# One gathered tile of rows in every third chunk fetched row by row from ScalarE's queue

## The reference

```
f = (x @ W_ni.T)[src] + (x @ W_nj.T)[dst] + e @ W_fij.T
f = leaky_relu(f, negative_slope=0.2)
score = f @ attn
m = segment_max(score, dst)
a = exp(score - m[dst])
a = a / segment_sum(a, dst)[dst]
h_out = segment_sum((x @ W_node.T)[src] * a, dst)
```

## Time and profile before

| | |
|---|---|
| median of three executions | 2192.31 us |
| the profiled execution's own time | 2185.84 us |
| its span (first to last instruction) | 2184.0 us |
| PE busy | 1812.9 us (83%) |
| POOL busy | 1588.6 us (73%) |
| DVE busy | 1497.5 us (69%) |
| ACT busy | 421.8 us (19%) |
| TensorE's mean granted clock | 0.929 |
| bytes moved | 486.65 MB, mean 223 GB/s |

### The profile page before, as it was taken

One profiled execution on the slowest core, in us unless ns is written; L12 is line 12 of the kernel. 1 busy time (PEld: TensorE's weight loads), 2 busy tenths in 40 slices (PEclk: granted clock), 3 DMA queues, 4 the chain that ended last, 5 costly groups with the idle time before them and its releaser, 6 DMA issues.

```text
span 2184.0 us, 43046 instructions
## 1 busy us (share of the span) xinstructions
PE 1812.9 (83%) x10541; PEld 1243.9 (57%) x10696; DVE 1497.5 (69%) x5518; ACT 421.8 (19%) x844; POOL 1588.6 (73%) x1671
## 2 busy tenths in 40 slices
PE   5699889888888888888857788888788888878887
PEld 3366666555565666555634555555555555555566
DVE  6488888777777767777735666666666667657666
ACT  2221121111111111111111112222212222222221
POOL 7777777777777777777277777777777777777771
PEclk9899999998999889999979999999999999999988
DMA  9889998888888878888456666666666666666661
GB/s 318 258 269 279 281 288 279 260 251 250 266 253 259 253 244 263 258 255 255 141 172 189 192 200 196 195 198 196 192 199 195 195 193 200 194 189 203 195 198 44
DMA packets 349544, 486.65 MB, mean 223 GB/s; under 512 B 114284, under 2 KB 215188, under 8 KB 349454
## 3 DMA queue, kind: packets, MB, share of 16 engines
q1 hardware_dynamic: 236515, 248.47, 37.7%
q0 software_dynamic: 78752, 213.75, 33.7%
q10 hardware_dynamic: 34203, 23.55, 3.6%
HBM read 407.69 MB, written 81.38 MB: 224 GB/s over the span
## 4 chain that ended last, share of the span: by engine, by line
POOL 54%; issue 18%; PE 14%; DMA 6%; DVE 5%; ACTq 1%; POOLq 1%; DVEq 1%; ACT 0%; SPq 0%
POOL xsrc L516 54%; PE pair L761 4%; PE bSC L750 4%; PE pair L719 2%; DMA xsrc<-h_table,idx_slot 2%; DMA xsrc<-x_table,idx_slot 2%; DMA proj<-xsrc 2%; PE pair L730 1%; ACTq L551 1%; DVE amat L1055 1%; PE pair L734 1%; DVE fT L1168 1%; DVE h L1171 0%; PE pair L722 0%; PE bXT L795 0%
## 5 line engine op out<-in xcount | busy, mean ns | idle before, releaser
L516 POOL DMA_INDIRECT xsrc<-h_table,idx_slot x831 | 792.4, 954 | 295.8 <-issue 249.6
L516 POOL DMA_INDIRECT xsrc<-x_table,idx_slot x767 | 731.4, 954 | 234.5 <-issue 226.7
L622 ACT ACTIVATE zc<-pair 128x512 f32<-128x512 f32 x416 | 248.4, 597 | 1584.2 <-PE pair L734 1004.8
L719 PE MATMUL pair<-edge_in,wts 128*128 128x512 f32 x832 | 483.8, 665 | 18.6 <-DMA window<-proj 18.4
L730 PEld LDWEIGHTS pair<-ident,xsrc 128*128 128x128 f32 x1600 | 195.8, 149 | 527.9 <-DMA xsrc<-h_table,idx_slot 294.4
L750 PE MATMUL bSC<-fT,attn_at 128*32 128x128 f32 x3328 | 480.3, 292 | 17.2 <-issue 3.9
L1168 DVE TENSOR_TENSOR fT<-pair,zc 128x512 f32<-128x512 f32 x416 | 285.6, 687 | 267.7 <-ACT zc L622 266.7
L730 PE MATMUL pair<-ident,xsrc 128*128 128x128 f32 x1600 | 273.7, 297 | 234.4 <-DMA xsrc<-h_table,idx_slot 162.2
L761 PEld LDWEIGHTS pair<-amat,xsrc 128*128 128x128 f32 x3328 | 426.5, 198 | 63.2 <-issue 50.8
L761 PE MATMUL pair<-amat,xsrc 128*128 128x42 f32 x3328 | 458.9, 290 | 2.5 <-DVE amat L1051 2.3
L750 PEld LDWEIGHTS bSC<-fT,attn_at 128*32 128x32 f32 x3328 | 350.8, 116 | 112.4 <-issue 96.4
(11 more groups left out here) (148 smaller groups left out, 1273.2 us busy)
## 6 DMA issues: line engine op xcount, KB each, us to landing
edge_in<-eT SPq DMA_DIRECT2D x208, 256.0 KB
rel_bc<-relrow_g SPq DMA_DIRECT2D x416, 128.0 KB
h1T<-h SPq DMA_DIRECT2D x208, 256.0 KB
edge_in<-h1T SPq DMA_DIRECT2D x208, 256.0 KB
window<-proj SPq DMA_DIRECT2D x416, 32.0 KB
xsrc<-h_table,idx_slot POOLq DMA_INDIRECT x831
xsrc<-x_table,idx_slot POOLq DMA_INDIRECT x767
hx<-xT SPq DMA_DIRECT2D x48, 121.0 KB
```

Source lines behind the costliest of these rows:

```text
L516: pool.indirect_dma_start(xsrc[b][:, i, 0:width], None, table, bass.IndirectOffsetOnAxis(ap=idx_slot[b][:, i:i + 1], axis=0)).then_inc(L.g ...
L622: nc.scalar.mul(zc[s][:, :], bZ[s][:, :], SLOPE).then_inc(L.z_scaled, 1)
L719: mm(bZ[s][:, :], fij, edge_in[q][:, :], start=True, stop=False)
```

## The change

The last tile (number 31) of the chunks 5, 8, 11, ..., 23 is no longer gathered by POOL, in both layers. That is 7 tiles a layer, 14 in all. ACT collects these rows instead:

- A host array `idxR` holds the 7 x 128 source numbers. ACT fetches one line of it into `line` (one partition, 128 integers).
- In the two and a half chunks ahead of an aided chunk ACT reads, at the end of each of its slots, some of these numbers into registers, and issues one transfer for each: one row of the table, 1 KB, into one partition of the tile `stage`. How many in which slot is given by `ROWS_AT`: 49 a chunk; the 128 rows are 7 in the last slot of one chunk, 49 and 49 in two whole chunks, and 23 in the third.
- In slot 6 of the third chunk ACT waits for the 128 landings, and copies `stage` by one transfer into the tile's place in `xsrc[2]`. In slot 7 it waits until that has landed, and begins the next round with 7 rows.
- PE waits in `z_sum` of the aided group for this copy as well as for the three gathered tiles.
- The four `window` buffers of 3 KB a partition become two, each used for two slots when, as here, the narrow path is taken. Their use in the narrow path is unchanged otherwise.

The core of the diff:

```diff
+AIDED = (CH - XB) // XB
+AID_AT = 2 * XB - 1
+ROWS_AT = {1: [3, 5, 4, 8, 8, 7, 7, 7], 2: [5, 7, 5, 6, 7, 6, 6, 7]}
+
+def first_row(n, turn, g):
+    counts = ROWS_AT[n]
+    before = 0 if turn == 0 else counts[GC - 1] + (turn - 1) * sum(counts)
+    at = before + (0 if turn == 0 else sum(counts[0:g]))
+    return at, max(0, min(counts[g], P - at))
...
-                        for i in range(g * TG, g * TG + TG - (SHORT if ends else 0)):
+                        aided = not isinstance(c, int) and b == AID_AT % XB and g == GC - 1
+                        for i in range(g * TG, g * TG + TG - (SHORT if ends else aided)):
...
+                def aided_rows(turn, u, begins, c, g):
+                    if turn == 2 and g == GC - 3 and begins:
+                        act.dma_start(line[:, :], idxR[bass.ds(u + 1, 1), :]).then_inc(L.line_in, 16)
+                    if turn == 2 and g == GC - 2 and reached(u, 0):
+                        act.wait_ge(L.rows_in, u * (16 * P) + 16 * P)
+                        act.wait_ge(L.num_made, c * GC - GC)
+                        act.dma_start(xsrc[AID_AT % XB][:, TC - 1, :], stage[:, :]).then_inc(L.aided_in, 16)
+                    if turn == 2 and g == GC - 1 and begins:
+                        above(act, L.aided_in, u * 16 + 16)
+                        act.wait_ge(L.line_in, u * 16 + 32)
+                        act.sem_inc(act_passed, 1)
+                    turn, begun = (0, begins) if turn == 2 and g == GC - 1 else (turn + 1, reached(u, 0))
+                    at, count = first_row(L.n, turn, g)
+                    if not begun or count == 0:
+                        return
+                    _, rows = nc.values_load_multi_w_load_instructions(
+                        line[0:1, at:at + count], engines=(ACT_,), min_val=0, max_val=N - 1,
+                        skip_runtime_bounds_check_because=IN_RANGE)
+                    for p, row in enumerate(rows):
+                        act.dma_start(stage[at + p:at + p + 1, :], L.table[bass.ds(row, 1), :]).then_inc(L.rows_in, 16)
...
-                for c in range(4):
-                    turn(c, True, c >= 1)
-                with act.Fori(4, CH - 1) as c:
-                    turn(c, True, True)
-                turn(CH - 1, True, True)
+                turn(1, True, True, (2, -1, True))
+                turn(2, True, True, (0, 0, False))
+                turn(3, True, True, (1, 0, False))
+                with act.Fori(0, AIDED - 1) as j:
+                    turn(j * XB + 4, True, True, (2, j, True))
+                    turn(j * XB + 5, True, True, (0, j + 1, False))
+                    turn(j * XB + 6, True, True, (1, j + 1, False))
...
-                        pe.wait_ge(L.gathered[b][g], uses * (16 * TG) - 16 * short)
+                        if b == AID_AT % XB and g == GC - 1:
+                            above(pe, L.aided_in, rounds * 16)
+                            pe.sem_inc(pe_passed, 1)
```

More of the change, by code:

```diff
@@ L29 @@
 SHORT = NT - TILES
+AIDED = (CH - XB) // XB
+AID_AT = 2 * XB - 1
+IN_RANGE = "src lies in [0, N)"
+ROWS_AT = {1: [3, 5, 4, 8, 8, 7, 7, 7], 2: [5, 7, 5, 6, 7, 6, 6, 7]}
[4 more added lines that the diff above has]
+    return at, max(0, min(counts[g], P - at))
 class Layer:
@@ L121, in program @@
     ALU, ACT = mybir.AluOpType, mybir.ActivationFunctionType
-    PE_, DVE_, SP_ = mybir.EngineType.PE, mybir.EngineType.DVE, mybir.EngineType.SP
+    DVE_, SP_, ACT_ = mybir.EngineType.DVE, mybir.EngineType.SP, mybir.EngineType.Activation
     proj = [nc.dram_tensor(f"proj{n}", [NP, 3 * D], bf16, kind="Internal").ap() for n in (1, 2)]
@@ L173, in program @@
         edge_in = [sb(f"edge_in{g}", [P, W]) for g in range(GS)]
-        window = [sb(f"window{g}", [P, 3 * TG, P], bf16) for g in range(GS)]
+        window = [sb(f"window{g}", [P, 3 * TG, P], bf16) for g in range(GS // 2)]
+        stage = sb("stage", [P, 2 * P])
+        line = sb("line", [1, P], i32)
         rel_bc = [sb(f"rel_bc{g}", [P, W], bf16) for g in range(GS)]
@@ L424, in chunk @@
                         if narrow:
-                            sp.dma_start(window[q][:, 0, :], L.proj.rearrange("n (h d) -> (n h) d", h=3)[
+                            sp.dma_start(window[q % 2][:, q // 2, :], L.proj.rearrange("n (h d) -> (n h) d", h=3)[
                                 bass.ds(first[g], P), :]).then_inc(L.loaded[q], 16)
@@ L428, in chunk @@
                             first = first_nodes(base_row, n * TG, TG, N)
+                            above(sp, L.z_made, n - 1)
+                            sp.sem_inc(sp_passed, 1)
                             for i in range(TG):
-                                sp.dma_start(window[q][:, 3 * i:3 * i + 3, :].rearrange("p h d -> p (h d)"),
+                                sp.dma_start(window[q % 2][:, 3 * i:3 * i + 3, :].rearrange("p h d -> p (h d)"),
                                              L.proj[bass.ds(first[i], P), :]).then_inc(L.loaded[q], 16)
@@ L616, in layer, with slot @@
             def layer(L, narrow):
-                def slot(c, g, front, soft):
+                def slot(c, g, front, soft, aid):
                     n, s = c * GC + g, g % 2
@@ L637, in slot @@
                         copy_rows(n + 1, 1 - s)
+                    if aid is not None:
+                        aided_rows(*aid, c, g)
+                def aided_rows(turn, u, begins, c, g):
[18 more added lines that the diff above has]
+                        act.dma_start(stage[at + p:at + p + 1, :], L.table[bass.ds(row, 1), :]).then_inc(L.rows_in, 16)
                 def copy_rows(n, s):
@@ L642, in copy_rows, with turn @@
                     nc.scalar.copy(xsT[s][:, :], bXT[:, :]).then_inc(L.xt_copied, 1)
-                def turn(c, front, soft):
+                def turn(c, front, soft, aid=None):
                     for g in range(GC):
-                        slot(c, g, front, soft)
+                        slot(c, g, front, soft, aid)
                 def whole_slab(k):
@@ L658, in layer @@
                     copy_rows(0, 0)
-                for c in range(4):
-                    turn(c, True, c >= 1)
-                with act.Fori(4, CH - 1) as c:
+                turn(0, True, False)
+                if L.n == 1:
+                    act.wait_ge(x_copied, 32)
+                    for q in range(4):
+                        act.wait_ge(p_ni_stored[q], 16 * slot_uses[q])
+                turn(1, True, True, (2, -1, True))
[5 more added lines that the diff above has]
+                    turn(j * XB + 6, True, True, (1, j + 1, False))
+                c = (AIDED - 1) * XB + 4
+                turn(c, True, True, (2, AIDED - 1, False))
+                for c in range(c + 1, CH):
                     turn(c, True, True)
-                turn(CH - 1, True, True)
                 turn(CH, False, True)
@@ L727, in z_sum @@
                             short = SHORT * (L.n - 1 + (isinstance(c, int) and c == CH - 1))
-                        pe.wait_ge(L.gathered[b][g], uses * (16 * TG) - 16 * short)
+                        if b == AID_AT % XB and g == GC - 1:
+                            above(pe, L.aided_in, rounds * 16)
+                            pe.sem_inc(pe_passed, 1)
+                            earlier = (L.uses_before[b] + 1) * (16 * TG) - 16 * AIDED * (L.n - 1)
+                            pe.wait_ge(L.gathered[b][g], rounds * (16 * (TG - 1)) + earlier)
+                        else:
+                            pe.wait_ge(L.gathered[b][g], uses * (16 * TG) - 16 * short)
                         for i in range(TG):
@@ L733, in z_sum @@
                     if narrow:
-                        last = mm(bZ[s][:, :], window[q][:, 0, :], onehot[s][:, :], start=False, stop=True)
+                        last = mm(bZ[s][:, :], window[q % 2][:, q // 2, :], onehot[s][:, :], start=False, stop=True)
                     else:
@@ L737, in z_sum @@
                             for part in range(3):
-                                mm(bZ[s][:, i * P:i * P + P], window[q][:, 3 * i + part, :],
+                                mm(bZ[s][:, i * P:i * P + P], window[q % 2][:, 3 * i + part, :],
                                    onehot[s][:, i * P:i * P + P], start=False, stop=False, skip_group_check=True)
```

8 lines of the change are left out of this document (6 added, 2 removed).

## The result

The changed kernel takes 2204.20 us (median of 6, 2198.57 to 2208.80), the kernel before 2190.86 us beside it (6, 2188.00 to 2192.45): ratio 1.0062 [1.0051, 1.0072], slower by 0.6% where 0.7% faster was forecast. A second set of runs gave 2202.20 against 2190.07 us, 1.0047 [1.0031, 1.0063]. Ten of the eighteen experiments ran on a chip where the kernel before takes 2816 to 2850 us, and they are told apart from the eight on chips where it takes 2190.

The account below looks back on a forecast made before the run. POOL was taken to set the pace at 1.258 us a gather: -17.6 us for 14 gathers, +1.5 early loss, gives -16.1, so 2169.7 against the profiled execution or 2176 against the median; range 2172 to 2255.

Parts of the forecast that it names:

- What goes: POOL, both layers: 14 gathers of 1.258 us disappear, saving 17.6 us, 8.8 in each layer.
- The condition: To keep the whole gain, a three-chunk round may take 115.6 us in layer 1 and 121.6 in layer 2.
- ACT's round in layer 1, 110.5 us: ACT's queue over three chunks of layer 1: rows, loads and other work sum to 110.5 us, below POOL's 119.5.
- the rival's 1.54 a load: Register load time on ACT above which, at 116.9 us a layer 1 round, ACT decides; forecast load 1.25 us.
- the forecast's other terms (17.7): ACT's layer 1 round besides rows and loads: dispatch 3.6, load-free slots 1.2, other work 8.4, line and copy 1.5, exponential.
- The early loss: Start of layer 1, chunks 2 and 3, POOL close behind PE's buffers: a late ACT costs 1.5 us.
- The DMA engines: Row transfers raise layer 1's DMA share from 0.85 to about 0.88; time unchanged while POOL sets the pace.
- The sixteen pieces for one row: Each 256-float row transfer splits into sixteen 64-byte pieces, about 66 us on each of 16 DMA engines.
- The register load's floor of about 600 ns: ACT's register loads at the documented floor alone would make rounds 14 us shorter, the forecast sum unchanged.
- ACT becomes the bound: Rival, chance 0.27: slow register loads or rows make ACT set the pace, 2220 to 2300 us.
- its +28: Rival's case with register loads of 1.7 us on ACT: rounds of 120.4 and 123.3 us, 2220 us total.
- signs of being wrong: POOL idle until PE in layer 1, DVE's ReLU waiting far longer for `zc`, and third, `zc` never waiting for PE.

Follow-up runs that it names:

- e15: Changed kernel with ACT collecting nothing and POOL still gathering 14 tiles less (output wrong): 2171.14 us, 0.9916 of the kernel before.
- e11: Changed kernel with each slot's rows fetched in one transfer of adjacent rows, register loads unused and absent from the trace (other output): 2171.39 us, 0.9914 of the kernel before.
- e14: Changed kernel with the register loads moved ahead of the slot's `zc`, ACT's loop kept: 2212.26 us, 1.0105 of the kernel before.
- e12: Changed kernel with the register loads ahead of `zc` and ACT's loop written out: 2173.64 us, 0.9919 of the kernel before.
- e13: Changed kernel with only ACT's loop written out, loads still behind `zc`: 2173.14 us, 0.9941 of the kernel before.
- e10: Changed kernel without register loads, single-row transfers from fixed table rows (other output): 2172.93 us, 0.9924 of the kernel before.

## Why the prediction was wrong

By its steps:

- *What goes*: right. A pitch of 1.258 us, 14 gathers fewer, 17.6 us, all of it there in e15 and e11.
- *The condition*: right. The chunks 23 and 24 take 67.8 us where 68 were taken. With the measured rounds its rule "7 x (round - 115.6) - 8.8" gives for chunk 25 +24.8 us in the changed kernel (measured 1044.9 - 1019.7 = +25.2), +36.0 in e14 (+37.4) and -1.8 in e12 (-0.4). Layer 2, which may take 121.6 us, ran at 119.8 in spite of pauses of 3.6 to 4.1 us: hidden, and 7.8 of the 8.8 us kept.
- *ACT's round in layer 1, 110.5 us*: the step that failed; it was 120.4. Its terms: a row takes 0.39 us within a slot and the first of a slot 0.65, so 128 rows are 56.4 us, not 65.3. Loads 22 x 1.62 = 35.6 us, not 27.5; the rival's 1.54 a load as the point of decision was passed, but the cheap rows paid for that, and e13 and e12 with the same loads win. Both together are 92.0 us where 92.8 were forecast: right by luck, since the two errors cancel. What was missing is another kind of term.
- *Missing, and decisive*: the branch back. A body of three chunks with 49 rows each was costed as if written out. It pauses ACT 2.5 to 3.9 us at each branch of layer 1, and the loop costs 4.6 us a round in all (e13), which is the distance between 115.8, just at the allowed 115.6, and 120.4. Three quarters of that lies in the chunks with the pause (24.0 of 32.6 us), the rest is spread over all chunks.
- *Missing, not decisive alone*: waits inside ACT's slots. The sum let every idle moment count for the rows, but ACT's queue is in order: a slot can't begin before its pair is made. In the slots that hold only the line or the copy of `stage` ACT has next to nothing to do and waits for PE. ACT's timeline in the changed kernel, with its idle time before each `zc`:

```profile
610.89 0.60 ACT L642 ACTIVATE zc<-pair 128x512 f32<-128x512 f32 x1 [2.79 <-remote]
611.04 0.23 ACTq L663 DMA_DIRECT2D line<-idxR  x1
614.48 0.60 ACT L642 ACTIVATE zc<-pair 128x512 f32<-128x512 f32 x1 [3.00 <-PE pair L794]
614.64 0.51 ACTq L667 DMA_DIRECT2D xsrc<-stage  x1
618.48 0.60 ACT L642 ACTIVATE zc<-pair 128x512 f32<-128x512 f32 x1 [3.40 <-PE pair L794]
```

  3.00 - 0.23 and 3.40 - 0.51 are 5.7 us of waiting in two slots, for which the sum had 1.2. In e13 the same two waits are 5.3 us in the mean. With the forecast's other terms (17.7) and the rows and loads measured in e13 (57.0 and 36.6) its round should be 111.3 us; it was 115.8. The waits give 5.3 - 1.2 = 4.1 of these 4.5 us.
- *The early loss* in chunks 2 and 3, 1.5 us: much too small. Chunk 5 starts at 248.0 instead of 237.9, 10.1 us later (e10, without the loads: 237.3). It is not an extra in the end, as layer 1's threshold counts the sum of all rounds.
- *The DMA engines*: right. A share of 0.85 as before, and 5628 packets more for 1792 rows and 14 copies. The sixteen pieces for one row, which the prediction worked out from the Trainium skill, "DMA: Bandwidth & Descriptors", section "Why a DMA increments its semaphore by 16 and not by 1", are not borne out: they would have made 28672 packets for the rows alone. The trace has 3584 more packets of 1 KB, one for each of the 1792 rows and of the 14 x 128 of the copies. e11, with 301 transfers instead of 1792 for the same bytes, has the same 39831 packets.
- *The register load's floor of about 600 ns* (the Trainium skill, "DMA: Bandwidth & Descriptors", section "Latency and other measured facts") agrees: the shortest was 657 ns. It was no guide to the mean of 1.62 us.

Of the rivals, "ACT becomes the bound" came about, at 120.4 us, but neither by a load like DVE's nor by a dear row. Its price for layer 1 fits, 7 x (120.4 - 115.6) - 8.8 = +24.8 us; its +28 for the same round in layer 1 has layer 2 above its bound too, which it was not. Of the signs of being wrong, POOL's and DVE's waits came in part (22.7 us after 11.1, 329.8 after 266.7), but not the third: `zc` still waits for PE, 628.3 us in 181 places. The chances listed add up to 0.65 for faster and 0.27 for slower, where the text has 0.64 and 0.28.

## What to carry to other kernels

Count the instructions in an engine's loop body before costing a change that puts register moves and small transfers into it: here a branch back over 540 instructions cost 2.5 to 4.1 us of nothing each time, over 262 it cost 0.3. The profile shows the fetch as a packet of the instruction queue within the pause. An in-order queue whose work is tied to another engine's steps can't be summed over a round; what it has to do must be set against each slot, and the time left over in light slots is lost (5.3 us a round here). That the new work takes less time than the pace-setting engine is not enough if that engine started with a lead: the followers must eat up the lead before the stage ends, so here 115.6 us a round were allowed and not 119.5.

## What was not expected of the hardware

- The pause at the branch: 2.5 to 5.0 us, ended about 1.6 us after one 8 KB packet of the instruction queue starts, and no longer with a body twice the size (3.2 and 4.0 in layer 1, 3.4 and 1.7 in layer 2).
- Single-row transfers of 1 KB from registers take 0.235 us each in ACT's queue and come 0.39 us apart within a slot, faster than the 0.48 of two stores, and each is one packet of 1 KB.
- Pauses of POOL of mostly 1.8 or 2.6 us instead of 0.30 on one chip, on which the kernel before took 2816 to 2850 us instead of 2190; their cause stays open.
